# Borders between three passes of a two-layer decoder: weights loaded in parts, a fold moved into the filling of pass 1, experts released before their loads are issued

## What is computed

```python
x = x + _L0_attn_ref(_layernorm(x), w_q, w_k, w_v, w_o)         # 16 heads of 16, 4 kv heads, rms norm, rope, tanh cap 50, causal
x = x + _L0_xattn_ref(_layernorm(x), ctx, ctx, Wq, bq, ...)     # 16 heads of 64; causal, so only ctx[:, 0:112] counts
x = x + _L0_ffn_ref(_layernorm(x), W1, b1, W2, b2, scale)       # 1024 wide, exact gelu, plus scale * token products m1, m2
x = x + _L1_attn_ref(_layernorm(x), wq, wk_down, wv_down, wk_up, wv_up, wo)   # 8 heads of 128, 2 kv heads, latent 32
x = x + _L1_xattn_ref(_layernorm(x), ctx, mask, qn_w, ..., Wo, bo)            # its own layernorms with weights, 16 heads of 16, masked
x = x + _L1_ffn_ref(_layernorm(x), ...)                         # 2 of 4 experts per sequence, each a whole encoder layer, weighted
```

## Time and profile before

| | us |
|---|---|
| median of 3 runs | 3741.29 |
| lowest, highest | 3738.55, 3749.99 |
| the profiled execution's own time | 3746.19 |
| its span (first to last instruction) | 3744.5 |
| TensorE busy | 3393.0 (91%) |
| DVE busy | 2125.9 (57%) |
| ScalarE busy | 1948.2 (52%) |
| GpSimd busy | 377.1 (10%) |

### The profile page before, as it was taken

The page is one execution under the profiler, slowest core; times in us unless marked ns, Lnnn a source line. Parts: engine busy times, 40 slices in busy tenths (PEclk is TensorE's granted clock), DMA queues, the critical chain, the costliest instruction groups (busy, mean ns, idle before and its releaser), DMA issues. The chain is left out here.

```text
span 3744.5 us, 81272 instructions
## 1 busy us (share of the span) xinstructions
PE 3393.0 (91%) x30471; PEld 2533.5 (68%) x30471; DVE 2125.9 (57%) x6898; ACT 1948.2 (52%) x6531; POOL 377.1 (10%) x455
## 2 busy tenths in 40 slices
PE   6999999998699899999999999973999989999997
PEld 4777777776466565656565656633887877877886
DVE  3666666666255454545455554522666666766765
ACT  2555555555144444444444444422666666666664
POOL 1111111111000000000000000000111111111111
PEclk8999999999699999999999999965999999999998
DMA  2000000000200000000000000004000011010000
GB/s 78 13 12 16 12 12 16 12 16 6 90 17 17 21 17 21 17 21 17 23 14 23 14 24 14 7 6 174 15 11 12 16 52 53 16 52 12 16 11 10
DMA packets 63549, 94.38 MB, mean 25 GB/s; under 512 B 7762, under 2 KB 59602, under 8 KB 62146
## 3 DMA queue, kind: packets, MB, share of 16 engines
q1 hardware_dynamic: 55074, 83.41, 7.0%
q0 software_dynamic: 8224, 7.36, 1.7%
HBM read 72.07 MB, written 18.37 MB: 24 GB/s over the span
## 5 line engine op out<-in xcount | busy, mean ns | idle before, releaser
L1232 DVE CUSTOM_DVE_ANT_0 PON<-pps,PMR 112x375 f32<-112x375 f32 x512 | 259.9, 545 | 305.8 <-PE pps L952 304.9
L1465 PE MATMUL bps<-BXT,Bwexp 128*128 128x112 f32 x3072 | 382.2, 283 | 26.7 <-SPq L1386 12.7
L1465 PEld LDWEIGHTS bps<-BXT,Bwexp 128*128 128x128 f32 x3072 | 369.2, 198 | 46.1 <-ACT BXT L1554 16.8
L1571 ACT ACTIVATE BPT<-bps,Blow 112x112 f32<-112x112 f32 x1024 | 346.8, 381 | 38.4 <-DVE Blow L1686 38.4
L1085 ACT ACTIVATE PPT<-pps,mcol 125x896 f32<-125x896 f32 x192 | 193.0, 1005 | 198.9 <-PE pps L971 198.6
L1571 ACT ACTIVATION_READ_ACCUMULATOR BPT<-bps,Blow 112x1 f32 x1024 | 241.1, 235 | 0.0
L952 PE MATMUL pps<-PKT,PQM 64*112 64x375 f32 x1024 | 227.1, 521 | 10.0 <-DVE Pmx L1232 7.9
L1536 PE MATMUL bps<-Bwexp,BPT 128*112 128x256 f32 x1024 | 235.2, 381 | 0.1
L655 POOL TENSOR_TENSOR rstd<-var,nhalf 112x1 f32<-112x1 f32 (+1 forms) x96 | 148.3, 1545 | 771.3 <-DVE var L573 535.2
L1265 POOL TENSOR_TENSOR Prstd<-Pvar,nhalf 112x1 f32<-112x1 f32 x128 | 71.6, 560 | 1450.8 <-DVE Pvar L1152 1450.8
L498 ACT ACTIVATE PT<-PT,low 112x112 f32<-112x112 f32 x512 | 191.2, 387 | 43.5 <-DVE low L630 43.3
(11 more groups left out here) (287 smaller groups left out, 7442.3 us busy)
## 6 DMA issues: line engine op xcount, KB each, us to landing
Bwexp<-in_we SPq DMA_DIRECT2D x7, 2304.0 KB, 13.8
PCX<-in_ctx SPq DMA_DIRECT2D x32, 375.0 KB
BXIN<-xmid SPq DMA_DIRECT2D x64, 112.0 KB
out<-BY POOLq DMA_DIRECT2D x64, 112.0 KB, 2.9
Bwexp<-in_we SPq DMA_DIRECT2D x7, 777.0 KB, 4.5
wa_sb<-in_wa SPq DMA_DIRECT2D x1, 4736.0 KB, 14.4
Brexp<-in_re SPq DMA_DIRECT2D x7, 672.0 KB
XIN<-in_x SPq DMA_DIRECT2D x32, 112.0 KB
```

What stands on the lines that cost most here:

```text
L1232: m = v.tensor_tensor_reduce(out=ON[s][0:T, i * LC:(i + 1) * LC], in0=bank[s][i][0:T, 0:LC], in1=MR[s][:, :], scale=1.0, scalar=-3.0e38, o ...
L1465: m = mm(o[:, j * T:(j + 1) * T], wt[:, c, n0 + j * 128:n0 + (j + 1) * 128], rhs[:, c, :], start=(c == 0), stop=(c == 1))
L1571: m = A(PT[s][0:T, h, :], bank[s][i][0:T, v * T:(v + 1) * T], ACT.Exp, scale=0.25, bias=low[s][:, h:h + 1], accum_out=sums[s][:, h:h + 1])
```

## The change

- Loading in pass 1: x and context tiles of the first items are issued first, then the weights in three parts, `xo` (`weights_mid`), `qkv0`, `o0`, `xk` (`weights_in`), and `xv`, `xq` (`weights_late`). TensorE waits for each part at its first use, in the filling only (`at.first`). The column order of `wa` is changed to suit.
- In the loop of pass 1 the context tile of the next item is loaded with its x tile, and `go` waits for both; the load at the head of the batch and its semaphore are gone.
- `csel`, `MV` and their DMAs are gone.
- The fold stands in pass 1, in the generators `fold` (TensorE) and `keep` (DVE). The filling calls the next of their steps every 20 places from place 400 on, and the rest before the loop. The loads for it (`up` in nine parts, and the Wq, Wk, Wv part `wy`) are issued before the first `go`. To make room, the tiles QT share memory with QM, and ON is narrower.
- Border of passes 1 and 2: SyncE issues the row tile, four x tiles, four context tiles, then the weights of pass 2 without the folded part in two loads. TensorE waits for these two before the first product of the second step.
- Border of passes 2 and 3: `routed` is raised after the four `go_last`, ahead of the expert loads; these have one register load for the early part and the row tile together, and one for the late part.
- `run_slots` has the tables FIRST and LAST for filling and draining in place of turns worked out from the leads. Their places are the same (a place of lane s in the filling is its turn less the lead plus 1000, in the draining its turn less the lead, not under 0).

```diff
-WA_PARTS = [("qkv0", C2 * 384), ("o0", C2 * D), ("xq", C2 * DFF), ("xk", C2 * DFF), ("xv", C2 * DFF), ("xo", FT * D),
+WA_PARTS = [("qkv0", C2 * 384), ("o0", C2 * D), ("xk", C2 * DFF), ("xv", C2 * DFF), ("xq", C2 * DFF), ("xo", FT * D),
...
+FIRST = {
...
+    "pe1": ((),
+            (753, 797, 803, 878, 878, 933, 962, 980,),
...
+    for turn in range(SPAN):
+        for s in lanes:
+            if lead[s]:
+                work(s, first[s], turn, before[s])
+        if turn >= 400 and turn % 20 == 0:
+            next(others, None)
+    for _ in others:
+        pass
...
+                for s in reversed(LANES):
                     sp.dma_start(XIN[s][:, :], x[s * quarter, :, :]).then_inc(x_in[s], 16)
-
+                    sp.dma_start(CX[s][:, :], ctx[s * quarter, 0:T, :]).then_inc(x_in[s], 16)
+                a, b, c = WA["xv"][0], WA["xo"][0], WA["yo"][0]
+                sp.dma_start(w[:, b:n1], wa[:, b:n1]).then_inc(weights_mid, 16)
+                sp.dma_start(w[:, 0:a], wa[:, 0:a]).then_inc(weights_in, 16)
+                sp.dma_start(w[:, a:b], wa[:, a:b]).then_inc(weights_late, 16)
+                sp.dma_start(XT[0][:, 0, 0:64], up[:, 0:64]).then_inc(prep_dma, 16)
+                for part in range(4):
+                    k = 64 + part * 1024
+                    sp.dma_start(upw[part], up[:, k:k + 3 * D]).then_inc(prep_dma, 16)
+                    sp.dma_start(upx[:, part, :], up[:, k + 3 * D:k + 4 * D]).then_inc(prep_dma, 16)
+                sp.dma_start(wy[:, :, :, :].rearrange("p k c n -> p (k c n)"), wa[:, WA["yq"][0]:c]).then_inc(prep_dma, 16)
+                for s in reversed(LANES):
+                    sp.wait_ge(x_in[s], 32)
+                    sp.sem_clear(lane_range[s]).then_inc(go[s], 1)
...
+                def fold(at):
+                    pe.wait_ge(prep_dma, 10 * 16)
+                    for h in range(8):
+                        part, k = h // 2, h % 2
+                        for c in range(C2):
+                            mm(bank[0][0][:, (c * 8 + h) * 32:(c * 8 + h) * 32 + 32], upw[part][:, k * D + c * 128:k * D + c * 128 + 128],
+                               upc, start=True, stop=True)
+                        yield
...
+                        yield
+                    for _ in range(5):
+                        yield
+                    pe.wait_ge(all_prepared, 2)
...
+                    for _ in range(12):
+                        yield
+                    pe.wait_ge(all_prepared, 3)
+                    pe.wait_ge(weights_in, 16)
+                    pe.wait_ge(weights_late, 16)
...
+                def keep(at):
...
+                    for _ in range(12):
+                        yield
+                    dve.wait_ge(prep, 2)
+                    v.tensor_copy(wqa[:, :, :].rearrange("p c n -> p (c n)"), bank[0][0][:, 0:C2 * D])
+                    v.tensor_copy(woa[:, :, :].rearrange("p c n -> p (c n)"), bank[0][1][:, 0:C2 * D])
+                    dve.drain().then_inc(all_prepared, 1)
+                    for _ in range(9):
+                        yield
+                    dve.wait_ge(prep, 3)
...
+                        pe.wait_ge(loaded, 7 * 16)
                     for c in range(C2):
                         mm(b1[0:96, 64:64 + T], XT[s][:, c, 1:97], XT[s][:, c, :], start=(c == 0), stop=(c == 1), skip_group_check=True)
...
                     sp.sem_clear(slot_sems[s]).then_inc(go_last[s], 1)
-                    load_early(s, 0)
-                    load_rows(s, 0)
+                sp.sem_inc(routed, 1)
                 for s in reversed(LANES):
-                    load_late(s, 0)
-                sp.sem_inc(routed, 1)
+                    e = sp.value_load(items[0:1, bass.ds(NI + s * (share + 1) + 1, 1)], min_val=0, max_val=E - 1)
+                    sp.dma_start(wexp[s][:, 0:early], we[bass.ds(e, 1), :, 0:early].rearrange("a p n -> (a p) n")).then_inc(c_in[s], 16)
+                    sp.dma_start(rexp[s][:, :], re_[bass.ds(e, 1), :].to_broadcast((T, NRE))).then_inc(m_in[s], 16)
+                for s in reversed(LANES):
+                    e = sp.value_load(items[0:1, bass.ds(NI + s * (share + 1) + 1, 1)], min_val=0, max_val=E - 1)
+                    sp.dma_start(wexp[s][:, early:NWE], we[bass.ds(e, 1), :, early:NWE].rearrange("a p n -> (a p) n")).then_inc(late_in[s], 16)
```

267 lines of the change are left out of this document (128 added, 139 removed), and 115 rows, old and new, of tables (FIRST, LAST).

## The result

| | before | after |
|---|---|---|
| median of 5 runs, us | 3738.55 | 3704.15 |
| lowest, highest | 3737.77, 3749.99 | 3699.34, 3714.30 |
| the profiled execution's own time | 3746.19 | 3714.30 |
| its span | 3744.5 | 3712.6 |
| mean granted clock | 0.953 | 0.960 |

The ratio is 0.9908, with an interval of 0.9885 to 0.9932: faster by 0.7 to 1.2%, 34 us by the medians and 31.9 by the two profiled executions. Predicted were 3702 us and a gain of 39.7. To see where the 31.9 us lie, both spans are cut at the same seven places of the program. The sum of the differences is the difference of the spans.

What follows compares the result with a forecast made beforehand. Four stretches where TensorE has little useful work (start, filling, two borders) were taken to bound the gain: 6.4 + 13.5 + 19.8 = 39.7 us off, so 3706.5 profiled, 3702 against the median; range 3687 to 3718.

Steps and rivals of the forecast that it cites:

- Start: Kernel start up to TensorE's first transposes: reordered loads bring them from 29.36 to 17.0 us, 12.4 us earlier.
- xo is there at 11.0: Start: the xo load (1.05 MB, 2.5 us) lands at 11.0 us, behind eight x and context tiles (2.2 us).
- The rival of the stuck issues: Start and border 1/2: SyncE's DMA issues get stuck, go comes at 19.9, border gives 11.6; sum 35, 3706 us; chance 0.08.
- the mark set for it: Start: TensorE's first transposes at 20 us or more, instead of 17, would show that issues got stuck.
- Fold: Filling of pass 1: the moved fold costs 5 us for TensorE, mostly hidden in 13.6 us idle, and 1 for DVE.
- start and filling together: Kernel start through lane 0's first transposes: 12.4 - 6 = 6.4 us gained, bounds -10 and +24.
- Border 1/2: Border of passes 1 and 2: without the fold, the first product on transposed x comes 13.5 us sooner, at 993.2.
- the 13.5 us for the context: Border of passes 1 and 2: four context loads, 1.54 MB at 114 GB/s, take 13.5 us, to 986.4.
- The lower end of the bounds, 11.6: Border of passes 1 and 2: 11.6 us gained if weights are issued only when all context has landed.
- Border 2/3: Border of passes 2 and 3: earlier release and expert loads bring the first expert product 19.8 us sooner; bounds 14 and 21.
- Loop: Loop of pass 1: moving the context load to the next x tile's load gains 0 us.
- The slow rival: Loop of pass 1: go waits for two loads, costing 2.0 us in each of 32 batches, 64 us, 3766; chance 0.03.

Runs made afterwards that it cites:

- xo_first: Changed kernel with pass 1's go ahead of the up and wy loads, and xo loaded right behind lane 3's x and context tiles; ratio 0.9900.
- best: Changed kernel with early go and earlier xo load, border 1/2 context loads split into 120 and 5 partitions, weights behind lane 3's context alone; ratio 0.9856.
- go_early: Changed kernel with SyncE's waits for x and the go signals of pass 1 ahead of the up and wy loads; first transposes at 22.07 us, ratio 0.9890.
- cx_split: Changed kernel with each context load at border 1/2 issued as two, of 120 and 5 partitions; border 19.52 us, ratio 0.9902.
- before_release: Kernel before, with only TensorE's release at border 2/3 moved ahead of the expert loads; border 12.03 us, ratio 0.9978, and 0.9947 when timed again.

## Why the prediction was right, and where its terms were not

- **Start: the mis-sized term.** 12.4 us were forecast, 7.2 came, and 7.1 to 8.3 in the six other profiles with the same start. The step that failed is "xo is there at 11.0": the sum moved the tiles and xo at 424 GB/s. The tiles were through 1.1 us later than in the sum, xo took 2.5 us more behind them, and the product began 0.3 us after xo's last packet. These are the 3.9 us by which it was late. Moving xo ahead of three lanes' tiles (xo_first) brought its product to 12.18, and to 11.61 in best, so the tiles ahead of it cost some 3 us, of which their low rate explains 1; why xo itself took so long stayed open. The other 1.3 us are the product, 6.43 us for 5.07, because more of it ran at 1.2 GHz; the prediction took its time over from a row in which the clock had risen earlier. The rival of the stuck issues was half right: the issues did get stuck (5.06 us) and the first transposes came after 20, the mark set for it, but go_early shows that in the changed kernel the go was not what they waited for.
- **Fold: near in size, not in mechanism.** 5 + 1 us were taken; 6.7 came in the profile, 8.5 in the mean of six, and perhaps 4 with the loop behind. The prediction had 13 us of work (from 22.3 at 1.2 GHz, a sum of overlapping groups), most of it hidden in TensorE's idle time. The work was 8.8 us, and 8.7 to 10.3 in the six profiles, and nearly all of it lies in sight: TensorE's idle time shrank by about 1 us. That less work and less hiding nearly cancel is luck. So start and filling together, with 6.4 us forecast, gave nothing: lane 0 begins at 97.3 to 101.5, and at 97.5 to 99.5 in the three profiles without the change. What the fold's new place earns, it earns at the border.
- **Border 1/2: right in mechanism, 3.4 us too high.** The context loads held the weights back, as predicted, and cx_split confirms the divisor of 125. The mis-sized term is the 13.5 us for the context, which put its end 17.8 us after the row tile's issue; it was 20.2, and 20.0 to 20.9 in the five other profiles with this order. The rate of 114 GB/s held only until the weights joined in; then a context packet took 82 to 85 ns for 48. The weights' part on those engines came 7.0 us behind (6.3 in the sum) and the product 0.8 (0.5): 2.4 + 0.7 + 0.3 = 3.4. The lower end of the bounds, 11.6, was not low enough for the 10.1 measured. The Trainium skill (DMA: Bandwidth & Descriptors, "Why a DMA increments its semaphore by 16 and not by 1") gives the rule of the divisor, by which 120 partitions get 15 engines. The share of 1.01 in cx_split, for 0.34 with 125, agrees. The same page of the Trainium skill ("Rules for kernel authors") says that one should not bother to make two transfers of the two halves of the partitions, because both halves run on all 16 engines. Here, with a load of 125 partitions, the split took 8.5 us off the border; no run splits a load of 128.
- **Border 2/3: right.** 18.4 for 19.8; before_release, with the release alone, gave 18.7. The weights took 5.7 us to land instead of 4.5. Nothing behind was late: the waits for Bwexp beyond the first are 11.0 us, as they were before (11.3).
- **Loop: 0 predicted, -4.1 in one profile,** mostly by dips of the clock, which come and go between profiles of one kernel (763.5 and 767.1 us in the two of the changed one). The slow rival (the go waits for two loads) is refuted: it would have added 64 us.
- **The total.** Against its own profiled execution the sum was 7.8 us too good (3706.5 for 3714.3): the start, fold, borders and pass 3 gave 5.2 + 0.7 + 3.4 + 1.4 + 1.5 = 12.2 us less than forecast, and the other stretches 4.4 more, of which 4.1 are the loop. The medians lie closer, 3702 and 3704.15, because the other executions of the changed kernel were mostly shorter than the profiled one; the gain of 34.4 us by medians is still 5 short of the 39.7. The kernel before had a median of 3738.55 beside the changed one, not the 3741.29 that the forecast started from; from 3738.55 the same sum gives 3699. So 2.7 us of the closeness are luck.
- **Where the gain lies.** The two borders give 28.5 of the 31.9 us, and the loop's clock 4.1; what start and filling gave and took is 0.5, and pass 3 took 1.5 more.

## What to carry to other kernels

Before putting a load in front of another, look at how many DMA engines it runs on (the DMA share) and at how many GB/s it moves at full share; both may be far from the rate of a large load, and what is queued behind pays. Release consumers before issuing bulk loads, since issues take the issuing engine's time, 0.4 us each here and several microseconds once they are stuck. Work that is moved into a filling is not hidden by the idle time there: of 9 to 10 us of products 6 to 11 were seen, and TensorE idled as long as before.

## What the runs showed of the hardware

- Tiles in pieces of 1 KB moved at 242 and 267 GB/s with all DMA engines busy, large weight rows at 426 to 429. A 1 KB packet took 48 ns while only the context's five engines worked (share 0.34), 60 to 67 ns with all engines at such packets, and 82 to 85 ns beside the packets of 18.9 KB of w.
- A DMA issue on SyncE takes 0.43 us while the queues are short and up to 13.21 us for three issues when 3.8 MB are ahead. Four context loads of 125 partitions took 7.18 us to issue; the same data as eight loads, of 120 and of 5 partitions, took 3.14 us.
- The loop of pass 1 takes 763 to 773 us for the same instructions of TensorE, by one to seven dips to 1.2 GHz, 1.6 us each. A single profile does not size a term of 4 us in a long stretch; a border of 30 us is read to 1 us.
